# Selective scan in groups of three units: two inputs, then three scans on VectorE

## The chip, the cores and the metric

The kernel runs on one core of a Trainium2 chip. The metric is the time of one execution in microseconds (us) on the device. Engines are named as in the profile: PE (TensorE), DVE (VectorE), ACT (ScalarE), POOL (GpSimd) and SP, whose queue issues the DMAs here.

## What is computed

The reference is a block of four parts on an input of 4 images of 32x32 tokens with 384 channels: a convolution with a selective scan (four directions, 192 channels, 16 states), an attention without softmax, a router, and a mixture of eight experts. The change touches only the selective scan:

```python
dA = jnp.exp(d_t[..., None] * As)
h = h * dA + (d_t * u_t)[..., None] * B_t[:, :, None, :]
y = jnp.einsum('bkcn,bkn->bkc', h, C_t)
```

`h` runs along the 1024 positions of an image, for each channel and each of the 16 states apart; `y` sums `h * C` over the states.

## The kernel before

All parts are written with explicit semaphores, and each engine's order is written out by hand. The scan stage is a loop over 12 **tiles** (`NQ`): a tile has 128 partitions (64 channels of two images) and 1024 positions. Tiles 1 to 10 are a loop on the engine, whose waits take their values from registers; tiles 0 and 11 are written out, with constants. A tile has 32 **units** (`UN`): two directions (`dr`) of 16 states (`n`). One unit goes through five engines:

- PE copies the unit's row of B over the partitions, two matmuls into one of two PSUM slots, `B_PS[u % 2]` (`spread(q, u, 0, ...)`, the matmul at L1040), and the row of C into `C_PS` (`spread(q, u, 1, C_PS)`, also L1040).
- ACT computes the decay, `exp(delta * A)` (L762), and copies C from PSUM to SBUF (L767).
- DVE multiplies B in its slot with `delta * x` (the **input**, L1503) and then scans (L1510).
- POOL multiplies h with C (the **readout**, L546) for two units in one instruction.
- PE adds that product into `Y_PS` with an identity matmul (L1056), `LAG` = 5 units later (`add_trailing_y`). The first add of a tile is preceded by a matmul of the skip weights (L1053), which waits until ACT has emptied the previous tile's sum (`evacuate_y`, L743) and has written the diagonal (`skip_weights`, L739).

Ten units of a tile, those with `n` in `ON_POOL` = (1, 4, 7, 10, 13), get their input otherwise: SP loads the row of B from DRAM into one of five `xin` buffers, POOL multiplies it (`make_input`, L529), and the decay goes into the PSUM slot that B would have had. They are **POOL units** here, the other 22 **DVE units**.

Buffers bound how far the engines run apart: a PSUM slot comes free with the scan two units before (the wait on `sc_ok` ahead of `spread`), `C_PS` with ACT's copy of the unit before (`c_free`), and one of eight `hst` buffers with the Y add of eight units before (`ya_ok`, ahead of each scan). Each engine's queue is in order. On PE the order of a unit is B (DVE units only), C, Y of the unit five before. On DVE it is input, scan, unit by unit. On POOL (`read_outs`) it is, for each pair of units, the inputs of the POOL units four and five ahead and then the pair's readout.

Of the kernel before, what the change touches and what calls it, by code (L numbers as in the profile page):

```python
# [5 lines left out]
ALU = mybir.AluOpType  # L6
# [7 lines left out]
B, HW, C, DI, N, R, K = 4, 32, 384, 192, 16, 24, 4  # L14
# [6 lines left out]
NP = B // 2  # L21
NQ = NP * 2 * J
# [5 lines left out]
UN = 2 * N  # L28
HALF = S // 2
HALVES = 2 * OJ  # L30
# [2 lines left out]
DRING = 2  # L33
HRING = 8
LAG = 5
ON_POOL = (1, 4, 7, 10, 13)
LEAD = 4
XRING = 5
PADW = HW + 2
# [3 lines left out]
MADE = 4  # L43
# [40 lines left out]


def pool_units(u):
    return u // N * len(ON_POOL) + sum(n in ON_POOL for n in range(u % N))


POOL_UNITS = [u for u in range(UN) if u % N in ON_POOL]  # L90
VEC_UNITS = UN - len(POOL_UNITS)
assert VEC_UNITS % DRING == 0

# [19 lines left out]
def decay_slot(u):  # L113
    return (u - pool_units(u)) % DRING


def decay_before(u):

    vec = [v for v in range(-UN, UN) if v % UN not in POOL_UNITS]
    return vec[vec.index(u) - DRING]  # L120


assert len(POOL_UNITS) % XRING == 0

# [23 lines left out]
def hybrid_block_kernel(nc, a, out):  # L148
    with ExitStack() as ctx:
        def sem(name):  # L150
            return ctx.enter_context(nc.semaphore(name))
# [32 lines left out]
        dlt, dux = rb.take(2, S), rb.take(2, S)  # L184
# [26 lines left out]
        xin, decay = rs.take(XRING, S), rs.take(DRING, S)  # L211
        c_sb, hst = rs.take(RING, S), rs.take(HRING, S)
# [49 lines left out]
        def pair_of_banks(b):  # L262
            return ps[:, b:b + 2, :].rearrange("p b c -> p (b c)")
# [6 lines left out]
        B_PS = [pair_of_banks(0), pair_of_banks(2)]  # L270
# [24 lines left out]
        ab_ok, dm_st = sem("abs_ready"), [sem(f"delta_stored{i}") for i in range(MADE)]  # L295
        dl_ld, du_ld = [sem("delta_in0"), sem("delta_in1")], [sem("delta_x_in0"), sem("delta_x_in1")]
        rows_ok, rows_st, in_ok = sem("rows_copied"), [sem("rows_stored0"), sem("rows_stored1")], sem("input_on_pool")
# [4 lines left out]
        b_ok, c_ok, c_free, dec_ok = (sem(n) for n in ("b_spread", "c_spread", "c_copied", "decay_ready"))  # L302
        p1_ok, sc_ok, p2_ok, ya_ok, yev_ok = (sem(n) for n in ("input_ready", "scanned", "readout_ready", "y_added", "y_evacuated"))
# [32 lines left out]
        def settled(eng):  # L336


            eng.sem_inc(passed, 1)
# [3 lines left out]
        def _(sp):  # L343
# [50 lines left out]
            def load_delta(q, dr):  # L394
                sp.dma_start(dlt[:, dr], dl_dram[q * 2 + dr]).then_inc(dl_ld[dr], 16)
                sp.dma_start(dux[:, dr], du_dram[q * 2 + dr]).then_inc(du_ld[dr], 16)
# [20 lines left out]
            def b_row(q, u):  # L417
                dr, n = divmod(u, N)
                x = q * len(POOL_UNITS) + pool_units(u)
                if x >= XRING:  # L420
                    old_q, old = divmod(x - XRING, len(POOL_UNITS))
                    sp.wait_ge(sc_ok, old_q * UN + POOL_UNITS[old] + 3)
                for im in range(2):
                    sp.dma_start(xin[H2 * im:H2 * im + H2, x % XRING],
                                 b_dram[q // J, dr, im * N + n].partition_broadcast(H2)).then_inc(b_ld[x % XRING], 16)
# [5 lines left out]
            for i in range(MADE):  # L431
                sp.wait_ge(dm_st[i], NP * HALVES // MADE * 32)
            for U in range(NQ * UN):
                if U % N == FETCH_AT and N <= U < (2 * NQ - 1) * N:

                    half = U // N + 1
                    sp.wait_ge(sc_ok, U - FETCH_AT + 2)
                    load_delta(half // 2, half % 2)
                if U % UN in POOL_UNITS:
                    b_row(U // UN, U % UN)  # L440
                if U % (J * UN) == N and J * UN <= U < 3 * J * UN:
# [177 lines left out]
        def _(act):  # L619
# [87 lines left out]
            for p in range(NP):  # L707
# [13 lines left out]
                for s in range(HALVES + 1):  # L721
# [7 lines left out]
                    k, n = s // J + 1, s // J + 2  # L729
# [8 lines left out]
            def skip_weights(q):  # L738
                nc.scalar.activation(d_diag, ident, ACT.Identity, scale=d_sum[:, q % OJ, :]).then_inc(diag_ok, 1)  # L739

            def evacuate_y(q):
                act.wait_ge(ya_ok, q * UN + (UN + HRING))
                nc.scalar.activation(xy[:, q, :], Y_PS, ACT.Copy).then_inc(yev_ok, 1)  # L743

            def units(q, first, last):
                for u in range(UN):
                    dr, n = divmod(u, N)
                    U = q * UN + u
                    if n == 0:

                        act.wait_ge(dl_ld[dr], q * 16 + 16)

                    if u == LAG and not first:
                        evacuate_y(q - 1)
                        skip_weights(q)

                    held = u - 2 if n in ON_POOL else decay_before(u)
                    dst = B_PS[u % 2] if n in ON_POOL else decay[:, decay_slot(u)]
                    if not (first and held < 0):
                        act.wait_ge(sc_ok, q * UN + (held + 3))  # L760
                        settled(act)
                    nc.scalar.activation(dst, dlt[:, dr], ACT.Exp,  # L762
                                         scale=a_neg[:, q % OJ, dr, n:n + 1]).then_inc(dec_ok, 1)
                    act.wait_ge(c_ok, U + 1)

                    act.wait_ge(p2_ok, U + 1)
                    nc.scalar.activation(c_sb[:, u % RING], C_PS, ACT.Copy).then_inc(c_free, 1)  # L767
# [145 lines left out]
        def _(pe):  # L913
# [103 lines left out]
            for p in range(NP):  # L1017
# [9 lines left out]
                for s in range(HALVES):  # L1027
                    delta_product(p, s)
                    k, n = s // J + 1, s // J + 2
# [6 lines left out]
            def spread(q, u, m, dst):  # L1036

                dr, n = divmod(u, N)
                for h in range(2):
                    mm = pe.matmul(dst[:, h * 512:(h + 1) * 512], sel_lhs[0:BR, n],  # L1040
                                   bc[0:BR, q % OJ // J, dr, m, h * 512:(h + 1) * 512], start=True, stop=True)
                return mm
# [17 lines left out]
            def add_trailing_y(q, u, first):  # L1060
                if u >= LAG:
                    add_y(q, u - LAG)
                elif not first:
                    add_y(q - 1, UN - LAG + u)

            def tile_steps(q, first, last):
                if not first and not last:
                    pe.wait_ge(bc_ld, 16 * ((q + 1) // J + 1))
                for u in range(UN):
                    dr, n = divmod(u, N)  # L1070
                    U = q * UN + u

                    if n not in ON_POOL:
                        pe.wait_ge(sc_ok, U + 1)
                        spread(q, u, 0, B_PS[u % 2]).then_inc(b_ok, 1)
                    pe.wait_ge(c_free, U + 1)
                    spread(q, u, 1, C_PS).then_inc(c_ok, 1)
                    add_trailing_y(q, u, first)


            pe.wait_ge(ev_free, NP * FILLS)
# [244 lines left out]
        def _(dve):  # L1326
# [155 lines left out]
                        split_lo(p, k)  # L1482


            def scans(q, first, last):
                for u in range(UN):
                    dr, n = divmod(u, N)
                    U = q * UN + u
                    if n == 0:

                        dve.wait_ge(du_ld[dr], q * 16 + 16)
                    h, slot = hst[:, u % HRING], B_PS[u % 2]
                    if n in ON_POOL:
                        f, x = slot, xin[:, pool_units(u) % XRING]

                        dve.wait_ge(in_ok, q * len(POOL_UNITS) + (pool_units(u) + 1))
                        dve.wait_ge(dec_ok, U + 1)
                    else:
                        f, x = decay[:, decay_slot(u)], slot
                        seen = q * VEC_UNITS + (u - pool_units(u) + 1)  # L1500

                        dve.wait_ge(b_ok, seen)
                        nc.vector.tensor_tensor(x, x, dux[:, dr], ALU.mult).then_inc(p1_ok, 1)  # L1503

                        dve.wait_ge(p1_ok, seen)
                        dve.wait_ge(dec_ok, U + 1)
                    dve.wait_ge(ya_ok, U + 1)
                    if dr:
                        h, f, x = h[:, ::-1], f[:, ::-1], x[:, ::-1]
                    nc.vector.tensor_tensor_scan(h, f, x, 0.0, ALU.mult, ALU.add).then_inc(sc_ok, 1)  # L1510

            for i in range(MADE):
                dve.wait_ge(dm_st[i], NP * HALVES // MADE * 32)
            for k in range(2):
                dve.wait_ge(bc_st[k], K * NP // 2 * PLACED)
                dve.wait_ge(rows_st[k], K * NP // 2 * 16)
            scans(0, True, False)
            with nc.vector.Fori(1, NQ - 1) as q:
                scans(q, False, False)
            scans(NQ - 1, False, True)  # L1520

            def centre(c):
                dve.wait_ge(mean_ok, c + 1)
# [356 lines left out]
```

## Time and profile before

| | us |
|---|---|
| median of 3 runs (lowest to highest) | 2389.55 (2389.35 to 2389.83) |
| the profiled execution | 2390.58 |
| its span, first instruction to last | 2388.8 |
| busy in the span: PE, DVE, ACT, POOL | 2046.9, 1599.6, 1140.5, 1302.0 |

The profiled execution took 1.8 us more than its span and 1.0 us more than the median. The scan stage lies between about 302 and 1526 us of the span: a little over half of it. Busy time is the time in which an instruction of the engine runs; a row names the source line, and the idle time in front of it is put down to what released it.

### The profile page before, as it was taken

The numbers are of one execution on the slowest core, as the hardware profiler recorded it, in microseconds if no ns is written. First come the engines' busy times: TensorE is split into PE (matmuls) and PEld (weight loads), VectorE is DVE, ScalarE is ACT, GpSimd is POOL, SyncE is SP. The second block draws the span as 40 slices with busy tenths as digits, with TensorE's granted clock in tenths as the row PEclk, the third lists the DMA queues.
The fourth block names the chain that finished last, engine by engine and source line by source line (L and its number), as shares of the span: only waits on it lengthen the run. The fifth ranks groups of instructions, "written<-read, shape, count | busy, mean of one in ns | idle before, by whom it ended". The sixth has DMA issues, their size and how long they took to land.

```text
span 2388.8 us, 20259 instructions
## 1 busy us (share of the span) xinstructions
PE 2046.9 (86%) x5902; PEld 958.1 (40%) x5902; DVE 1599.6 (67%) x1480; ACT 1140.5 (48%) x1238; POOL 1302.0 (55%) x467
## 2 busy tenths in 40 slices
PE   6996578888888888888888888779997699999998
PEld 3432123333333333333333333236664355555554
DVE  5686989999999999999999999582556000000000
ACT  2684756666666666666666666312121111111111
POOL 0101079999999999999999999611222111111110
PEclk9987679999999999999999999899999899999999
DMA  5454533222333223233222231320223533333210
GB/s 213 173 192 124 217 80 109 76 61 61 75 88 88 70 61 75 66 97 83 61 61 61 81 95 36 159 88 8 74 86 128 199 118 119 119 116 119 98 43 6
DMA packets 78850, 231.98 MB, mean 97 GB/s; under 512 B 10783, under 2 KB 37009, under 8 KB 76880
## 3 DMA queue, kind: packets, MB, share of 16 engines
q1 hardware_dynamic: 72656, 214.39, 28.5%
q0 software_dynamic: 6144, 16.98, 2.0%
q8 instruction: 24, 0.39, 0.1%
q14 instruction: 26, 0.21, 0.0%
HBM read 169.24 MB, written 64.03 MB: 98 GB/s over the span
## 4 chain that ended last, share of the span: by engine, by line
PE 46%; DVE 32%; issue 12%; ACT 7%; DMA 1%; POOL 0%; DVEq 0%; ACTq 0%; SPq 0%; POOLq 0%
DVE arena L1510 18%; PE ps L1311 10%; PE ps L1299 10%; PE ps L1056 8%; DVE ps L1503 6%; PE ps L1040 3%; ACT ps L762 3%; PE ps L1247 3%; PE ps L955 2%; DVE arena L1385 1%; PE ps L1053 1%; PE ps L1198 1%; PE ps L1236 1%; PE ps L1176 1%; PE ps L982 1%
## 5 line engine op out<-in xcount | busy, mean ns | idle before, releaser
L546 POOL TENSOR_TENSOR arena<-arena 128x2048 f32<-128x2048 f32 x192 | 869.7, 4530 | 70.7 <-DVE arena L1510 70.6
L1056 PE MATMUL ps<-arena 128*128 128x512 f32 x1536 | 754.2, 615 | 3.3 <-POOL arena L546 3.2
L1510 DVE TENSOR_TENSOR_SCAN arena<-arena,ps 128x1024 f32<-128x1024 f32 x264 | 603.7, 2287 | 44.9 <-DVE ps L1503 23.5
L1040 PE MATMUL ps<-arena 96*128 (+1 forms) x1296 | 357.0, 391 | 209.1 <-DVE arena L1510 189.4
L767 ACT ACTIVATE arena<-ps 128x1024 f32<-128x1024 f32 x384 | 391.7, 1020 | 276.0 <-PE ps L1040 272.2
L1056 PEld LDWEIGHTS ps<-arena 128*128 128x128 f32 x1536 | 302.1, 197 | 268.0 <-issue 208.3
L529 POOL TENSOR_TENSOR arena<-arena 128x1024 f32<-128x1024 f32 x120 | 283.4, 2362 | 98.0 <-DMA arena<-b_rows 98.0
L1040 PEld LDWEIGHTS ps<-arena 96*128 96x128 bf16 x1296 | 118.7, 99 | 537.2 <-DVE arena L1510 298.9
L1503 DVE TENSOR_TENSOR ps<-ps,arena 128x1024 f32<-128x1024 f32 x264 | 318.8, 1208 | 5.6 <-DMA delta_x<-arena 2.9
L1782 DVE TENSOR_TENSOR arena<-ps,arena 128x384 f32<-128x384 f32 x32 | 17.9, 558 | 449.2 <-PE ps L1311 449.2
L762 ACT ACTIVATE arena<-arena 128x1024 f32<-128x1024 f32 x264 | 301.2, 1141 | 24.6 <-DVE arena L1510 24.6
L1510 DVE TENSOR_TENSOR_SCAN arena<-ps,arena 128x1024 f32<-128x1024 f32 x120 | 271.8, 2265 | 3.6 <-POOL arena L529 3.6
L605 POOL DMA_INDIRECT out<-arena x32 | 31.8, 994 | 436.0 <-DVE arena L1787 436.0
L1311 PE MATMUL ps<-arena 128*128 128x384 f32 x768 | 250.1, 486 | 0.0
L1299 PE MATMUL ps<-arena 128*128 128x512 f32 x576 | 249.0, 593 | 0.0
L1311 PEld LDWEIGHTS ps<-arena 128*128 128x128 f32 x768 | 145.4, 190 | 101.6 <-issue 3.8
L762 ACT ACTIVATE ps<-arena 128x1024 f32<-128x1024 f32 x120 | 134.2, 1119 | 106.7 <-DVE arena L1510 106.7
L1299 PEld LDWEIGHTS ps<-arena 128*128 128x128 f32 x576 | 109.7, 191 | 136.1 <-issue 133.7
L891 ACT ACTIVATE arena<-ps,arena 128x512 f32<-128x512 f32 x96 | 66.1, 689 | 175.8 <-PE ps L1299 175.8
L578 POOL TENSOR_TENSOR arena<-arena 128x384 f32<-128x384 f32 x32 | 27.0, 877 | 203.2 <-DVE arena L1624 203.2
L898 ACT ACTIVATE arena<-arena 128x384 f32<-128x384 f32 x32 | 16.8, 525 | 232.3 <-DVE arena L1782 232.3
L517 POOL COPY arena<-arena 128x1024 f32<-128x1024 f32 x6 | 13.4, 2238 | 190.8 <-ACT arena L648 190.8
(202 smaller groups left out, 1669.3 us busy)
## 6 DMA issues: line engine op xcount, KB each, us to landing
arena<-b_rows SPq DMA_DIRECT2D x240, 256.0 KB, 7.5
arena<-in_w SPq DMA_DIRECT2D x16, 2304.0 KB, 16.6
delta<-arena SPq DMA_DIRECT2D x24, 512.0 KB, 2.9
delta_x<-arena SPq DMA_DIRECT2D x24, 512.0 KB, 3.7
arena<-delta SPq DMA_DIRECT2D x24, 512.0 KB, 3.6
arena<-delta_x SPq DMA_DIRECT2D x24, 512.0 KB, 4.5
arena<-in_xT SPq DMA_DIRECT2D x6, 1536.0 KB, 9.8
slot_in<-arena SPq DMA_DIRECT2D x8, 772.0 KB, 13.7
```

Of the source, the lines that this page charges most:

```text
L529: nc.gpsimd.tensor_tensor(xin[:, x % XRING], xin[:, x % XRING], dux[:, dr], ALU.mult).then_inc(in_ok, 1)
L546: nc.gpsimd.tensor_tensor(hst[:, h:h + 2], hst[:, h:h + 2], c_sb[:, c:c + 2], ALU.mult).then_inc(p2_ok, 2)
L762: nc.scalar.activation(dst, dlt[:, dr], ACT.Exp, scale=a_neg[:, q % OJ, dr, n:n + 1]).then_inc(dec_ok, 1)
L767: nc.scalar.activation(c_sb[:, u % RING], C_PS, ACT.Copy).then_inc(c_free, 1)
L891: nc.scalar.activation(h_sb[:, m], ps[:, 3 + m % 3, :], ACT.Gelu_apprx_tanh, bias=b1_col[:, e, m:m + 1]).then_inc(hg_ok, 1)
L1040: mm = pe.matmul(dst[:, h * 512:(h + 1) * 512], sel_lhs[0:BR, n], bc[0:BR, q % OJ // J, dr, m, h * 512:(h + 1) * 512], start=True, stop=True)
L1056: mm = pe.matmul(Y_PS[:, h * 512:(h + 1) * 512], ident, hst[:, u % HRING, h * 512:(h + 1) * 512], start=False, stop=(u == UN - 1))
L1247: mm = pe.matmul(ps[:, attend_bank(i), 0:CA], xnT[:, b % 2, t, i * P:(i + 1) * P], w_eff[:, t], start=(t == 0), stop=(t == CT - 1))
L1299: mm = pe.matmul(ps[:, 3 + m % 3, :], w1[s][:, t, m * P:(m + 1) * P], xeT[:, s, t], start=(t == 0), stop=(t == CT - 1))
L1311: mm = pe.matmul(ps[:, 6 + i % 2, 0:C], h_sb[:, m, i * P:(i + 1) * P], w2[s][:, m], start=(m == 0), stop=(m == MT - 1))
L1503: nc.vector.tensor_tensor(x, x, dux[:, dr], ALU.mult).then_inc(p1_ok, 1)
L1510: nc.vector.tensor_tensor_scan(h, f, x, 0.0, ALU.mult, ALU.add).then_inc(sc_ok, 1)
```

## The change

The POOL units of a tile become every third one, 2, 5, ..., 29: ten again, so 22 DVE units remain, of which 30 and 31 form a last group of two. DVE's program is cut in two functions. For each group of three it issues the inputs of both DVE units and then the three scans. PE follows: within a group it spreads B, C of the first unit, B of the second, then one Y add, C, Y add, C of the third, Y add. The number of instructions of each kind is what it was. `decay_slot`, `decay_before` and POOL's program are not edited, but follow `POOL_UNITS`. DVE's wait on the stored deltas ahead of the stage is gone (its first input still waits for `delta_x` to be loaded).

```diff
-ON_POOL = (1, 4, 7, 10, 13)
+GROUP = 3
...
 def pool_units(u):
-    return u // N * len(ON_POOL) + sum(n in ON_POOL for n in range(u % N))
+    return u // GROUP
...
-POOL_UNITS = [u for u in range(UN) if u % N in ON_POOL]
+POOL_UNITS = list(range(GROUP - 1, UN, GROUP))
...
-                    held = u - 2 if n in ON_POOL else decay_before(u)
-                    dst = B_PS[u % 2] if n in ON_POOL else decay[:, decay_slot(u)]
+                    held = u - 2 if u in POOL_UNITS else decay_before(u)
+                    dst = B_PS[u % 2] if u in POOL_UNITS else decay[:, decay_slot(u)]
...
-                    if n not in ON_POOL:
+                    at = u % GROUP
+                    if u not in POOL_UNITS:
                         pe.wait_ge(sc_ok, U + 1)
                         spread(q, u, 0, B_PS[u % 2]).then_inc(b_ok, 1)
+                    if at == 1:
+                        add_trailing_y(q, u - 1, first)
                     pe.wait_ge(c_free, U + 1)
                     spread(q, u, 1, C_PS).then_inc(c_ok, 1)
-                    add_trailing_y(q, u, first)
+                    if at:
+                        add_trailing_y(q, u, first)
...
-            for i in range(MADE):
-                dve.wait_ge(dm_st[i], NP * HALVES // MADE * 32)
...
+            def scans(q):
+
+                for g in range(0, UN, GROUP):
+                    units = range(g, min(g + GROUP, UN))
+                    for u in units:
+                        if u not in POOL_UNITS:
+                            input_of(q, u)
+                    for u in units:
+                        scan(q, u)
```

`input_of(q, u)` waits for B (`b_ok`) and multiplies; `scan(q, u)` has the waits and the scan of before.

In DVE's queue, in tile 0, from unit 0 on, before (L1503 is an input, L1510 a scan; the scan with `arena<-ps,arena` is that of a POOL unit):

```order
208 L1510 SCALAR_TENSOR_TENSOR arena<-arena,ps 128x1024 [waits y_added,decay_ready,input_ready]
209 L1510 SCALAR_TENSOR_TENSOR arena<-ps,arena 128x1024 [waits y_added,decay_ready,input_on_pool]
210 L1503 TENSOR_TENSOR ps<-ps,arena 128x1024 [waits b_spread]
211 L1510 SCALAR_TENSOR_TENSOR arena<-arena,ps 128x1024 [waits y_added,decay_ready,input_ready]
212 L1503 TENSOR_TENSOR ps<-ps,arena 128x1024 [waits b_spread]
213 L1510 SCALAR_TENSOR_TENSOR arena<-arena,ps 128x1024 [waits y_added,decay_ready,input_ready]
```

The same place now (L1496 is an input, L1513 a scan; the first row of tile 0 is input 0):

```order
208 L1496 TENSOR_TENSOR ps<-ps,arena 128x1024 [waits b_spread]
209 L1513 SCALAR_TENSOR_TENSOR arena<-arena,ps 128x1024 [waits y_added,decay_ready,input_ready] x2
210 L1513 SCALAR_TENSOR_TENSOR arena<-ps,arena 128x1024 [waits y_added,decay_ready,input_on_pool]
211 L1496 TENSOR_TENSOR ps<-ps,arena 128x1024 [waits b_spread] x2
212 L1513 SCALAR_TENSOR_TENSOR arena<-arena,ps 128x1024 [waits y_added,decay_ready,input_ready] x2
213 L1513 SCALAR_TENSOR_TENSOR arena<-ps,arena 128x1024 [waits y_added,decay_ready,input_on_pool]
```

No scan stands right behind its own input any more: another input lies between.

In PE's queue, in the loop's body, units 3 to 5 of a tile before (L1040 with `scanned` is B, with `c_copied` C; L1056 is a Y add):

```order
308 L1074 REGISTER_ALU
309 L1040 MATMUL ps<-arena 128x512 [waits scanned]
310 L1040 MATMUL ps<-arena 128x512
311 L1040 MATMUL ps<-arena 128x512 [waits c_copied]
312 L1040 MATMUL ps<-arena 128x512
313 L1054 REGISTER_ALU
314 L1056 MATMUL ps<-arena 128x512 [waits readout_ready]
315 L1056 MATMUL ps<-arena 128x512
```

And units 3 and 4 now:

```order
308 L1075 REGISTER_ALU
309 L1040 MATMUL ps<-arena 128x512 [waits scanned]
310 L1040 MATMUL ps<-arena 128x512
311 L1040 MATMUL ps<-arena 128x512 [waits c_copied]
312 L1040 MATMUL ps<-arena 128x512
313 L1075 REGISTER_ALU
314 L1040 MATMUL ps<-arena 128x512 [waits scanned]
315 L1040 MATMUL ps<-arena 128x512
316 L1054 REGISTER_ALU
317 L1056 MATMUL ps<-arena 128x512 [waits readout_ready]
318 L1056 MATMUL ps<-arena 128x512
```

B of the group's second unit has moved ahead of the Y add that used to stand before it, and all three Y adds of the group are queued behind its wait.

## Rows read from the trace of the kernel before

**Rows 1.** Window of 100 us: length, busy us (count) of PE, PEld, DVE, ACT, POOL, clock, DMA, GB/s
```profile
500.00:600.00 100.00, 84.38 (x238) 35.22 (x237) 95.68 (x55) 66.16 (x66) 94.03 (x26) 0.97 0.27 73
```
**Rows 2.** Groups of instructions, shapes apart: busy, mean ns | idle before, releasers
```profile
L546 POOL TENSOR_TENSOR arena<-arena 128x2048 f32<-128x2048 f32 x192 | 869.7, 4530 | 70.7 <-DVE arena L1510 70.6
L1510 DVE TENSOR_TENSOR_SCAN arena<-arena,ps 128x1024 f32<-128x1024 f32 x264 | 603.7, 2287 | 44.9 <-DVE ps L1503 23.5 <-ACT ps L762 15.1 <-PE ps L1056 3.8
L1503 DVE TENSOR_TENSOR ps<-ps,arena 128x1024 f32<-128x1024 f32 x264 | 318.8, 1208 | 5.6 <-DMA delta_x<-arena 2.9 <-PE ps L1040 2.7
L1510 DVE TENSOR_TENSOR_SCAN arena<-ps,arena 128x1024 f32<-128x1024 f32 x120 | 271.8, 2265 | 3.6 <-POOL arena L529 3.6
```
**Rows 3.** Timeline of DVE: the first scans of tiles 6 and 7
```profile
913.39 2.29 DVE L1510 TENSOR_TENSOR_SCAN arena<-arena,ps 128x1024 f32<-128x1024 f32 x1 [0.20 <-ACT ps L762]
1014.54 2.29 DVE L1510 TENSOR_TENSOR_SCAN arena<-arena,ps 128x1024 f32<-128x1024 f32 x1 [0.20 <-ACT ps L762]
```
**Rows 4.** Timeline of DVE in the loop: start, us, what, idle before
```profile
1000.15 1.21 DVE L1503 TENSOR_TENSOR ps<-ps,arena 128x1024 f32<-128x1024 f32 x1
1001.54 2.29 DVE L1510 TENSOR_TENSOR_SCAN arena<-arena,ps 128x1024 f32<-128x1024 f32 x1 [0.19 <-ACT ps L762]
1003.75 2.27 DVE L1510 TENSOR_TENSOR_SCAN arena<-ps,arena 128x1024 f32<-128x1024 f32 x1
1005.93 1.21 DVE L1503 TENSOR_TENSOR ps<-ps,arena 128x1024 f32<-128x1024 f32 x1
```
**Rows 5.** Timeline of DVE in tile 11, outside the loop
```profile
1424.39 1.21 DVE L1503 TENSOR_TENSOR ps<-ps,arena 128x1024 f32<-128x1024 f32 x1
1425.64 2.29 DVE L1510 TENSOR_TENSOR_SCAN arena<-arena,ps 128x1024 f32<-128x1024 f32 x1
```
**Rows 6.** Timeline of DVE ahead of the stage: two products independent of each other
```profile
294.93 1.22 DVE L1430 TENSOR_TENSOR arena<-arena 128x1024 f32<-128x1024 f32 x1
296.08 1.22 DVE L1423 SCALAR_TENSOR_TENSOR arena<-arena 128x1024 f32<-128x1024 f32 x1
```
**Rows 7.** Timeline at the stage's start: POOL's first inputs and unit 1's scan
```profile
307.54 4.64 POOL L529 TENSOR_TENSOR arena<-arena 128x1024 f32<-128x1024 f32 x2 [97.99 <-DMA arena<-b_rows]
309.92 2.29 DVE L1510 TENSOR_TENSOR_SCAN arena<-ps,arena 128x1024 f32<-128x1024 f32 x1 [3.62 <-POOL arena L529]
```
**Rows 8.** Timeline of PE in the loop: spreads (two pairs), Y add, spreads
```profile
1003.89 1.04 PE L1040 MATMUL ps<-arena 96*128 x4 [1.89 <-DVE arena L1510]
1004.76 1.88 PE L1056 MATMUL ps<-arena 128*128 128x512 f32 x4
1006.48 1.03 PE L1040 MATMUL ps<-arena 96*128 x4
```
**Rows 9.** Timeline at the change of tiles: ACT, PE, and DVE's wait behind them
```profile
1024.77 1.01 ACT L743 ACTIVATE arena<-ps 128x1024 f32 x1
1025.67 0.40 ACT L739 ACTIVATE arena<-arena 128x128 f32<-128x128 f32 x1
1025.96 1.15 ACT L762 ACTIVATE arena<-arena 128x1024 f32<-128x1024 f32 x1
1032.26 1.03 PE L1040 MATMUL ps<-arena 96*128 x4
1032.90 1.23 DVE L1503 TENSOR_TENSOR ps<-ps,arena 128x1024 f32<-128x1024 f32 x1 [0.91 <-PE ps L1040]
```
**Rows 10.** Timeline of POOL in the loop: readout, input, readout
```profile
1000.45 4.53 POOL L546 TENSOR_TENSOR arena<-arena 128x2048 f32<-128x2048 f32 x1 [0.61 <-DVE arena L1510]
1004.95 2.37 POOL L529 TENSOR_TENSOR arena<-arena 128x1024 f32<-128x1024 f32 x1
1007.27 4.52 POOL L546 TENSOR_TENSOR arena<-arena 128x2048 f32<-128x2048 f32 x1
```
**Rows 11.** Windows of 4 us in the loop, columns as in rows 1
```profile
848.00:852.00 4.00, 2.33 (x7) 0.86 (x5) 3.81 (x3) 3.10 (x3) 3.22 (x1) 1.00 0.00 0
852.00:856.00 4.00, 3.78 (x7) 1.66 (x8) 3.81 (x4) 2.06 (x2) 4.00 (x3) 0.59 0.00 0
```

More of the change, by code:

```diff
@@ L1482, in _ @@
                         split_lo(p, k)
[L1485 to L1510, printed above, removed]
@@ L1512, in _, with input_of, scan @@
-            for i in range(MADE):
-                dve.wait_ge(dm_st[i], NP * HALVES // MADE * 32)
+            def input_of(q, u):
+                dr, x = u // N, B_PS[u % 2]
+                seen = q * VEC_UNITS + (u - pool_units(u) + 1)
+                if u % N == 0:
+                    dve.wait_ge(du_ld[dr], q * 16 + 16)
+                dve.wait_ge(b_ok, seen)
+                nc.vector.tensor_tensor(x, x, dux[:, dr], ALU.mult).then_inc(p1_ok, 1)
+            def scan(q, u):
+                dr, U = u // N, q * UN + u
+                h, slot = hst[:, u % HRING], B_PS[u % 2]
+                if u in POOL_UNITS:
+                    f, x = slot, xin[:, pool_units(u) % XRING]
+                    dve.wait_ge(in_ok, q * len(POOL_UNITS) + (pool_units(u) + 1))
+                else:
+                    f, x = decay[:, decay_slot(u)], slot
+                    dve.wait_ge(p1_ok, q * VEC_UNITS + (u - pool_units(u) + 1))
+                dve.wait_ge(dec_ok, U + 1)
+                dve.wait_ge(ya_ok, U + 1)
+                if dr:
+                    h, f, x = h[:, ::-1], f[:, ::-1], x[:, ::-1]
+                nc.vector.tensor_tensor_scan(h, f, x, 0.0, ALU.mult, ALU.add).then_inc(sc_ok, 1)
@@ L1516, in _ @@
                 dve.wait_ge(rows_st[k], K * NP // 2 * 16)
-            scans(0, True, False)
+            scans(0)
             with nc.vector.Fori(1, NQ - 1) as q:
-                scans(q, False, False)
-            scans(NQ - 1, False, True)
+                scans(q)
+            scans(NQ - 1)
             def centre(c):
```

## The prediction

> **What bounds the kernel now.** I read the windows first: in 100 us of the stage DVE is busy 95.7 us, POOL 94.0, PE 84.4, ACT 66.2 [rows 1]. The groups then say who waits. DVE's scans were idle before for 44.9 us in all, and the row puts most of that down to DVE's own input (23.5) and to ACT's exp (15.1), while the inputs waited only 2.7 us for PE; POOL's readouts waited 70.6 us for DVE's scans [rows 2]. So DVE is the bound, and the others wait for it. The timeline shows what DVE's 101.15 us per tile [rows 3] are made of. From an input's start to its own scan's start 1.39 us pass in the loop [rows 4] and 1.25 in tile 11 [rows 5], though the input lasts 1.21. From a scan to the next instruction it is 2.21 or 2.18 us, less than the scan's 2.29 or 2.27 [rows 4]: an instruction that needs nothing of the one before starts 0.08 us before that one ends. 22 x 1.39 + 32 x 2.20 = 101.0 us, the tile's period. There is no other wait in a tile of the loop. The exp that rows 2 and 4 name ended just when the input did; it isn't a second cost, since the 1.39 is the same where ACT is not named.
>
> **The change, term by term.**
>
> 1. *The dependent start goes.* A scan now has another input between itself and its own. The trace before has no input followed by something independent of it; the bounds are the input's whole 1.21 us from above, and 1.21 less the overlap seen elsewhere, 0.07 for two independent products (296.08 - 294.93 = 1.15 of 1.22 us) [rows 6] to 0.08, from below. I take 1.14, since rows 6 are the same engine with an instruction nearly as short. Gain: 10 tiles x 22 x (1.39 - 1.14) = 55.0 us, and 2 x 22 x (1.25 - 1.14) = 4.8: **59.8 us**. With 1.21 it is 41.4, with 1.13 it is 62.5. The 0.14 us that the loop has over tile 11 I read as register work and further waits that come one after another once the input is done; now they can run under the second input.
>
> 2. *The first POOL unit.* Unit 1's scan waited 3.62 us for POOL's input, which began at 307.54 [rows 7]. Now unit 2 is the first; its input is ready at 309.9, as before. DVE was free at 306.3 after an input and a scan (1.25 + 2.2); now it does two of each first (2 x 1.14 + 2 x 2.2 = 6.7), and is free at 309.5. The wait shrinks to 0.4: **3.2 us gained**.
>
> 3. *The steady group, on the other engines.* A group takes DVE 2 x 1.14 + 3 x 2.20 = 8.9 us (9.4 before). Count from the end of the last scan of the group before. DVE starts its inputs at -0.1 and 1.05, the scans at 2.2, 4.4 and 6.6. B of the second unit, call it B2, needs the very scan that ends at 0. PE started 0.06 us after a scan's end (1001.54 + 2.29 to 1003.89) [rows 4, 8], and an input started 0.64 after its spread did (1032.90 - 1032.26) [rows 9]: B2 is usable at 0.70, wanted at 1.05. That holds if PE is free at 0. A pair of spreads takes 0.43 us, half of the 0.87 between rows 8's first starts, and a Y add 1.72 (1004.76 to 1006.48) [rows 8]. PE thus has B2 0.1 to 0.5, Y to 2.2, C to 2.6, Y to 4.4, C to 4.8, Y to 6.5, then the next group's first B when the second scan ends (6.7) to 7.2, and C to 7.6. It is idle until 8.9, 1.3 us to spare and 0.35 more before DVE waits. ACT's exp of the POOL unit waits for the scan that ends at 4.5 and takes 1.15 [rows 9] and is done at about 5.8, wanted at 6.6. Cost: nothing. If PE came later than those 1.65 us, DVE would wait for each us beyond.
>
> 4. *The change of tiles.* Before the third Y add of the second group stands the skip matmul, and it needs ACT's two steps, which need the old tile's last Y add. In that group the old tile's last Y starts at 2.6 and ends, 1.88 later [rows 8], at 4.5; ACT's L743 follows, L739 ends 1.30 us after L743's start and the next exp starts 1.19 after it [rows 9]. So PE gets the diagonal at 6.0, the skip matmul (like a Y add, 1.72) and the Y add go to 9.5, and B of the next group is usable at 10.15 where DVE wants it at 8.8. The exp of the third unit starts at 5.8 and ends at 6.9, 0.3 late, a part of the same wait. Before, such waits summed to 2.7 us in the stage [rows 2]. Eleven changes x 1.35 = **15 us lost**. Ends: 0, if LAG's slack takes it up, and 25.
>
> 5. *POOL.* Start to start a readout takes 4.50 us and an input 2.32 [rows 10]: 16 x 4.50 + 10 x 2.32 = 95.2 us per tile. DVE's tile becomes 22 x 1.14 + 32 x 2.20 + 1.35 = 96.8. Six units cost POOL 3 x 4.50 + 2 x 2.32 = 18.1 us and DVE 17.8: inside a tile POOL falls back 0.3 us per six units, 1.7 over thirty, and recovers over the last two units, which hold no POOL unit. PE's third Y add of each second group is the one that meets it, at 4.8; it may come at 6.5. Walked through, the readout is done at 5.0 early in the tile and 6.0 late. Cost 0, with half a us of air.
>
> 6. *The clock.* In some windows PE ran part of the time at half speed, the lower level of 1.2 GHz: the granted clock was 0.59 in one whose predecessor had PE busy only 2.33 of 4 us [rows 11]. A stretch of some 3 us costs PE 1.6 us, just the slack of term 3. I put **3 us** for those that fall on a tile's change. Idle stretches of PE get shorter, from 1.9 us [rows 8] to 1.3, so I expect no more of them.
>
> The dropped wait on stored deltas costs and gives nothing: the first input still waits for `delta_x` (2.9 us in rows 2), loaded after those stores. SP's row loads and delta loads are issued at the same units give or take one; five buffers are ten or more units ahead.
>
> Sum: -59.8 - 3.2 + 15 + 3 = -45.0 us. The profiled execution took 2390.6, which gives 2345.6; the median of the runs is 1.0 lower: **2345 us**.
>
> **Rivals.**
>
> *All of it arrives* (0.12). The change of tiles costs nothing: 2389.6 - 63.0 = 2327 us. For it: before, the inputs waited 2.7 us for PE in the whole stage [rows 2]. Against: term 4's chain is 1.3 us longer than its place.
>
> *POOL paces* (0.15). Scans now come in bursts, pairs do not fit triples, and POOL's readout idles now and then as it does now (101.15 - 95.2 = 6 us per tile). If half of that stays, a tile takes 98.2: 10 x 2.95 + 5 for the other two tiles + 3 = 37 us gained, 2352 us.
>
> *The start isn't set by the dependence* (0.06). An input would take 1.39 us to any successor, because DVE needs that time between two instructions of this kind; term 1 is then 0, term 4 shrinks to about 0.8 x 11 = 9, and the time is 2389.6 - 3.2 + 9 = 2395 us. Against it stand the 2.18 and 2.21 us after scans, with the same waits, and rows 6.
> The Trainium skill, "VectorE: DVE Perf Modes", section "The DRAIN you can't avoid", speaks for this one: the next operation waits until the pipe is empty whatever the semaphores do, so one should cut operations, not waits. By that rule reordering would bring nothing; the overlap of 0.08 us in rows 4 already disagrees with it.
>
> *PE comes late to B2, slower than before* (0.07). Place: the wait on the scan ahead of B2, with three Y adds behind it. If PE is still in a Y add when the scan ends, DVE's second input waits up to 1.72 - 0.35 = 1.4 us in each of 132 groups: 181 us, 2526 us. It decides from (59.8 + 3.2) / 132 = 0.48 us per group. A cause could be the clock: at half speed PE's three Y adds and five spread pairs take 2 x 7.3 = 14.6 us a group, against DVE's 8.9. Against it: the 1.3 us to spare.
>
> **How the numbers follow.** The forecast has 0.60; its own range is 2335 to 2356, from the ends of term 4 and a value of 1.17 in term 1. A measurement here tells 0.2% (4.8 us). The range that leaves out two in ten takes in the first rival and POOL's, and 1.21 in term 1: 2327 to 2366. Faster 0.88: the forecast, the first two rivals and a small part of the others. Same 0.03, slower 0.09.
>
> **What would show it.** Right: input to input and input to scan 1.13 to 1.15 us; a tile in the loop 96 to 98 us; DVE's idle before scans named by its own input nearly gone; a wait for PE of about 1 us at the input of unit 6, once a tile, and none at the second input of a group; POOL's idle before readouts down from 70 to about 20 us. Wrong: intervals near 1.39, waits at each group's second input, readouts without idle time and PE waiting for them, or a granted clock well under 0.97 in the stage.

## The result, and the profile after

| | before | after |
|---|---|---|
| median (lowest to highest), us | 2389.45 (2388.55 to 2389.83), 4 runs | 2348.74 (2346.89 to 2350.89), 4 runs |
| profiled execution, us | 2390.58 | 2349.24 |
| span, us | 2388.8 | 2347.4 |

The ratio is 0.9826 (95% interval 0.9813 to 0.9839): 41 us less, where 45 were forecast. The groups of instructions of the kernel after, columns as in [rows 2]:

```profile
L546 POOL TENSOR_TENSOR arena<-arena 128x2048 f32<-128x2048 f32 x192 | 865.9, 4523 | 2.9 <-DVE arena L1513 2.9
L1056 PE MATMUL ps<-arena 128*128 128x512 f32 x1536 | 732.5, 599 | 59.9 <-POOL arena L546 59.8
L1513 DVE TENSOR_TENSOR_SCAN arena<-arena,ps 128x1024 f32<-128x1024 f32 x264 | 587.9, 2268 | 0.0
L529 POOL TENSOR_TENSOR arena<-arena 128x1024 f32<-128x1024 f32 x120 | 283.0, 2358 | 128.9 <-DMA arena<-b_rows 128.9
L1496 DVE TENSOR_TENSOR ps<-ps,arena 128x1024 f32<-128x1024 f32 x264 | 309.9, 1219 | 28.5 <-PE ps L1040 28.2
L1513 DVE TENSOR_TENSOR_SCAN arena<-ps,arena 128x1024 f32<-128x1024 f32 x120 | 271.9, 2266 | 7.9 <-ACT ps L762 4.2 <-POOL arena L529 3.4 <-issue 0.4
```

The DVE units' scans (L1513, before L1510) had 44.9 us of idle time in front of them and now have none. The inputs (L1496, before L1503) had 5.6 and now have 28.5, nearly all for PE. On POOL things turned round: its readouts waited 70.7 us for DVE and now 2.9, but its inputs wait 128.9 us for the DMA of their rows, where they waited 98.0. Those 98 us are the time before the stage; the other 31 are new. PE's Y adds now wait 59.9 us for POOL, before 3.3. So POOL, which waited for DVE, is now waited for.

DVE in a steady group, the answer to [rows 4] (start, us, what; `x2` is two in a row):

```profile
916.80 2.34 DVE L1496 TENSOR_TENSOR ps<-ps,arena 128x1024 f32<-128x1024 f32 x2
919.05 4.46 DVE L1513 TENSOR_TENSOR_SCAN arena<-arena,ps 128x1024 f32<-128x1024 f32 x2
923.42 2.27 DVE L1513 TENSOR_TENSOR_SCAN arena<-ps,arena 128x1024 f32<-128x1024 f32 x1
925.60 2.34 DVE L1496 TENSOR_TENSOR ps<-ps,arena 128x1024 f32<-128x1024 f32 x2
```

The two inputs take 2.25 us from start to start of what follows, 1.13 each, and the group 8.80. Over the loop the means are 1.127 from an input to the next and 1.131 from an input to a scan; before, 1.404 from an input to its scan (1.244 in the two tiles outside the loop).

The change of tiles, the answer to [rows 9]:

```profile
902.23 1.02 ACT L743 ACTIVATE arena<-ps 128x1024 f32 x1 [0.81 <-PE ps L1056]
903.15 0.39 ACT L739 ACTIVATE arena<-arena 128x128 f32<-128x128 f32 x1
903.44 1.11 ACT L762 ACTIVATE ps<-arena 128x1024 f32<-128x1024 f32 x1
903.81 1.98 PE L1053 MATMUL ps<-arena 128*128 x4 [1.30 <-ACT arena L739]
904.59 2.29 DVE L1513 TENSOR_TENSOR_SCAN arena<-ps,arena 128x1024 f32<-128x1024 f32 x1 [0.42 <-ACT ps L762]
905.62 1.88 PE L1056 MATMUL ps<-arena 128*128 128x512 f32 x4
```
```profile
907.98 2.36 DVE L1496 TENSOR_TENSOR ps<-ps,arena 128x1024 f32<-128x1024 f32 x2 [1.10 <-PE ps L1040]
```

This is the chain of term 4: evacuation, diagonal, exp of unit 5, skip matmul, and DVE waits 0.42 us at the scan of unit 5 and 1.10 at the input of unit 6, 1.52 us in each tile of the loop.

What was not forecast stands ahead of it in the same tile. SP and POOL:

```profile
888.78 0.33 SPq L395 DMA_DIRECT2D arena<-delta  x1
889.14 0.43 SPq L396 DMA_DIRECT2D arena<-delta_x  x1
889.62 4.96 SPq L424 DMA_DIRECT2D arena<-b_rows  x8
890.76 4.51 POOL L546 TENSOR_TENSOR arena<-arena 128x2048 f32<-128x2048 f32 x1
897.69 2.36 POOL L529 TENSOR_TENSOR arena<-arena 128x1024 f32<-128x1024 f32 x1 [2.41 <-DMA arena<-b_rows]
900.01 9.00 POOL L546 TENSOR_TENSOR arena<-arena 128x2048 f32<-128x2048 f32 x2
```

The old tile's last scan ended at 888.75. The delta loads wait for it and went out at 888.78, and the row of B of unit 5 stands behind them in SP's queue. It was issued at 889.62, and POOL's input, which needs it, began at 897.69 after 2.41 us of idle time. At the start of each of the tiles 1 to 10 POOL's input began 8.4 to 9.8 us after that scan's end and had idled 1.9 to 3.7 us. Before, unit 4 was the POOL unit, issued ahead of the delta loads.

POOL never makes up for that wait: apart from the row it waits for nothing in the loop, and most tiles last its 95.0 us of work and its wait. Late in the tile its readouts come too late for PE, and PE for DVE. One of the longest such waits, at unit 30 of tile 2 (the last line is a window, columns as in [rows 1], the clock in it 0.75):

```profile
585.12 2.93 PE L1056 MATMUL ps<-arena 128*128 128x512 f32 x4 [1.80 <-POOL arena L546]
588.95 2.42 DVE L1496 TENSOR_TENSOR ps<-ps,arena 128x1024 f32<-128x1024 f32 x2 [1.79 <-PE ps L1040]
```
```profile
584.00:588.00 4.00, 2.88 (x5) 1.11 (x6) 3.16 (x2) 2.10 (x3) 4.00 (x2) 0.75 0.00 0
```

PE had stood idle for 1.80 us until 585.12; from 586.02 on the granted clock was at its lower level, 0.5 or 1.2 GHz, for a short stretch. DVE's waits for PE at the inputs of units 24 and 30 sum to 14.3 us in the stage, and the five of 1.5 us and more, 9.4 us of the 14.3, all lie at such a stretch; each of these five stretches began 0.4 to 1.2 us after the end of a wait of PE for POOL of 1.8 us. DVE's other waits at these two units last at most 0.4 us.

### The profile page after: what moved, and what is told of

It is laid out like the page before. It is cut to its first block, busy times and chain, and to the rows that moved or that the text cites. A ratio compares the mean times of both kernels' runs of the same rounds, so it can differ in the third digit from the quotient of the medians.

```text
span 2347.4 us, 20258 instructions
## 1 busy us (share of the span) xinstructions
PE 2031.5 (87%) x5902; PEld 940.8 (40%) x5902; DVE 1577.5 (67%) x1480; ACT 1141.0 (49%) x1238; POOL 1298.9 (55%) x467
## 3 DMA queue, kind: packets, MB, share of 16 engines
q1 hardware_dynamic: 72656, 214.39, 29.1%
## 4 chain that ended last, share of the span: by engine, by line
PE 46%; DVE 18%; issue 15%; POOL 14%; ACT 5%; DMA 1%; ACTq 0%; DVEq 0%; POOLq 0%; SPq 0%
PE ps L1315 11%; PE ps L1303 11%; DVE arena L1513 10%; POOL arena L546 9%; PE ps L1056 7%; POOL arena L529 5%; PE ps L1251 3%; PE ps L1040 2%; PE ps L955 2%; ACT arena L767 1%; DVE arena L1389 1%; DVE ps L1496 1%; PE ps L1053 1%; PE ps L982 1%; PE ps L1202 1%
## 5 line engine op out<-in xcount | busy, mean ns | idle before, releaser
L1056 PE MATMUL ps<-arena 128*128 128x512 f32 x1536 | 732.5, 599 | 59.9 <-POOL arena L546 59.8
L1513 DVE TENSOR_TENSOR_SCAN arena<-arena,ps 128x1024 f32<-128x1024 f32 x264 | 587.9, 2268 | 0.0
L1040 PE MATMUL ps<-arena 96*128 (+1 forms) x1296 | 366.6, 387 | 115.0 <-DVE arena L1513 94.0
L1056 PEld LDWEIGHTS ps<-arena 128*128 128x128 f32 x1536 | 287.8, 190 | 324.1 <-issue 193.8
L529 POOL TENSOR_TENSOR arena<-arena 128x1024 f32<-128x1024 f32 x120 | 283.0, 2358 | 128.9 <-DMA arena<-b_rows 128.9
L1496 DVE TENSOR_TENSOR ps<-ps,arena 128x1024 f32<-128x1024 f32 x264 | 309.9, 1219 | 28.5 <-PE ps L1040 28.2
L1040 PEld LDWEIGHTS ps<-arena 96*128 96x128 bf16 x1296 | 116.3, 99 | 444.0 <-issue 188.2
L1513 DVE TENSOR_TENSOR_SCAN arena<-ps,arena 128x1024 f32<-128x1024 f32 x120 | 271.9, 2266 | 7.9 <-ACT ps L762 4.2
L1303 PE MATMUL ps<-arena 128*128 128x512 f32 x576 | 249.0, 593 | 0.0
L1315 PEld LDWEIGHTS ps<-arena 128*128 128x128 f32 x768 | 145.4, 190 | 101.6 <-issue 3.8
L1303 PEld LDWEIGHTS ps<-arena 128*128 128x128 f32 x576 | 109.6, 191 | 136.1 <-issue 133.7
```

The costliest lines, as they stand in the source:

```text
L529: nc.gpsimd.tensor_tensor(xin[:, x % XRING], xin[:, x % XRING], dux[:, dr], ALU.mult).then_inc(in_ok, 1)
L1056: mm = pe.matmul(Y_PS[:, h * 512:(h + 1) * 512], ident, hst[:, u % HRING, h * 512:(h + 1) * 512], start=False, stop=(u == UN - 1))
L1303: mm = pe.matmul(ps[:, 3 + m % 3, :], w1[s][:, t, m * P:(m + 1) * P], xeT[:, s, t], start=(t == 0), stop=(t == CT - 1))
L1315: mm = pe.matmul(ps[:, 6 + i % 2, 0:C], h_sb[:, m, i * P:(i + 1) * P], w2[s][:, m], start=(m == 0), stop=(m == MT - 1))
```

## Experiments

All ran beside the kernel before, whose own median was 2389.4 to 2391.4 from one set of runs to the next, so that small differences are read from the ratios. The medians are of 4 to 10 runs each.

| run | median, us | ratio to before (95%) | loop tile, us |
|---|---|---|---|
| after (the change) | 2348.7 | 0.9826 (0.9813 to 0.9839) | 97.0 to 99.6 |
| rows first | 2333.4 | 0.9763 (0.9747 to 0.9779) | 96.4 |
| skip later | 2345.1 | 0.9807 (0.9791 to 0.9824) | 97.1 to 99.4 |
| both | 2317.8 | 0.9698 (0.9682 to 0.9714) | 95.2 |
| PE's old order | 2363.1 | 0.9890 (0.9874 to 0.9907) | 98.4 to 99.3 |
| units only | 2398.6 | 1.0029 (1.0018 to 1.0041) | 101.3 to 102.9 |
| wait back | 2351.1 | 0.9828 (0.9812 to 0.9844) | 96.5 to 99.2 |
| units, rows first | 2401.1 | 1.0033 (1.0020 to 1.0045) | 101.1 to 102.9 |
| both, PE old | 2357.4 | 0.9857 (0.9840 to 0.9873) | 98.3 |
| units, rows first, skip later | 2386.9 | 0.9991 (0.9981 to 1.0001) | 101.1 to 102.1 |
| both, PE old, skip with unit 3 | 2338.2 | 0.9781 (0.9763 to 0.9798) | 96.9 |

**Rows first.** SP's two steps of a unit change places:

```diff
 for U in range(NQ * UN):
+    if U % UN in POOL_UNITS:
+        b_row(U // UN, U % UN)
     if U % N == FETCH_AT and N <= U < (2 * NQ - 1) * N:
...
-    if U % UN in POOL_UNITS:
-        b_row(U // UN, U % UN)
```

> The changed kernel, but SP issues the row of B of unit 5 of each half tile ahead of the two delta loads instead of behind them. Theory (POOL paces: its tile is 95.2 us of work plus the 2 to 3.7 us that it waits for that row; its lag is what makes PE late at units 24 and 30): POOL's idle time put down to the row's DMA falls from 129 to about 98 us (the start alone), the 0.4 us waits of DVE for PE at the inputs of units 24 and 30 go, those of 1.5 to 2.1 us shrink, the tile falls from 97.3 to about 96.5 us, the time from 2349 to about 2336. Rival (those waits come from pairs against triples and from the clock, and the row only fills idle time): POOL idles elsewhere, tile 97.3, 2346 or more.

(The edit moves the row of unit 5 alone: the other delta loads are issued at unit 21, which has no row.) 15.3 us less than the change, and 2333.4 where about 2336 was expected. In the loop POOL no longer waits for a row, and DVE waits at the change of tiles alone (waits of DVE and of POOL, 400 to 1400 us: in total, times, longest):

```profile
DVE ps L1496 <- PE ps L1040: 11.9, 11, 1.1
DVE arena L1513 <- ACT ps L762: 4.2, 10, 0.4
```
```profile
POOL arena L546 <- DVE arena L1513: 13.1, 11, 1.2
```

The waits at units 24 and 30 are gone, the long ones too. The theory stands: they came from POOL's lag. The stretches of low clock went with them. The kernel after had four in the loop, this run has none, and its granted clock is 1.00 in the whole loop.

**Skip later.** The skip matmul joins the sum with unit 4, and ACT writes its diagonal one unit later:

```diff
+SKIP_AT = 4
...
-                if u == 0:
+                if u == SKIP_AT:
...
-                        pe.matmul(Y_PS[:, h * 512:(h + 1) * 512], d_diag, xy[:, q, h * 512:(h + 1) * 512], start=True, stop=False)
+                        pe.matmul(Y_PS[:, h * 512:(h + 1) * 512], d_diag, xy[:, q, h * 512:(h + 1) * 512], start=False, stop=False)
...
-                                   start=False, stop=(u == UN - 1))
+                                   start=(u == 0), stop=(u == UN - 1))
...
                         evacuate_y(q - 1)
+                    if u == LAG + 1 and not first:
                         skip_weights(q)
```

> The changed kernel, but the skip weights' matmul is added with unit 4 instead of ahead of unit 0, and ACT writes the diagonal one unit later. Both theories: the waits at the third scan and at the input of unit 6 (0.42 and 1.10 us a tile, 15 to 17 us in all) go nearly to zero. Theory (POOL paces the tile at 95.2 + 2.1 = 97.3): the time returns as waits at units 24 and 30, and the kernel gains under 4 us: 2345 to 2349. Rival (DVE's chain at the change of tiles is on the path): 2349 - 15 = 2334.

3.6 us less, and the ranges overlap (2340.6 to 2350.4 against 2346.9 to 2350.9); 2345.1 lies in the theory's range. The profiled execution is the slowest of the four. In it DVE's waits for PE did not shrink, they spread:

```profile
DVE ps L1498 <- PE ps L1042: 25.6, 37, 3.7
```
```profile
POOL arena L530 <- DMA arena<-b_rows: 30.9, 11, 3.9
POOL arena L547 <- DVE arena L1515: 0.8, 1, 0.8
```

The first row is of DVE, 25.6 us against 25.1 in the kernel after over the same 1000 us; the others are of POOL, which still waits for its row and for next to nothing else. Its own work is 95.0 us a tile, its wait for the row 2 to 4, and most tiles are their sum. The 1.10 us at unit 6 are gone from most tiles; waits of 0.3 to 0.4 us stand at units 12, 18, 24 and 30, and the longest, up to 3.7 us at unit 6 and 1.7 at unit 30, lie at the seven stretches of low clock in its loop. The times of its executions go with the clock: the mean granted clock was 0.954 in the slowest and 0.957 in the fastest. So the 3.6 us are a rough figure.

**Both.**

> Both edits of the two runs before. Theory (two bounds nearly equal, each hides the other): more than the sum of the single gains; tile at POOL's 95.2 to 95.7 us, time 2322 to 2328. Rival (they are independent): the sum of the single gains.

2317.8 us, 31.0 less than the change where the single gains add up to 18.9, and 3% less than the kernel before. The tile came out as expected, 95.2 us; the time lies 4 us below the expected range. This is the fastest version of the study, and its loop too has no stretch of low clock. A window of the stage, columns as in [rows 1]:

```profile
500.00:600.00 100.00, 87.32 (x252) 35.48 (x251) 99.83 (x58) 71.36 (x71) 99.89 (x29) 1.00 0.32 85
```

DVE and POOL are both busy all the time (99.8 and 99.9 us of 100): 22 x 1.13 + 32 x 2.19 = 94.9 us of DVE and 95.0 of POOL in a tile of 95.2. By these rows a shorter tile would need less work on both; that was not tried.

**PE's old order**, with DVE's groups kept:

```diff
-                    if at == 1:
-                        add_trailing_y(q, u - 1, first)
                     pe.wait_ge(c_free, U + 1)
                     spread(q, u, 1, C_PS).then_inc(c_ok, 1)
-                    if at:
-                        add_trailing_y(q, u, first)
+                    add_trailing_y(q, u, first)
```

> The changed kernel with PE's old order: B, C, Y add, unit by unit; DVE's groups are kept. By the walk through a group the Y add in front of the group's second B ends 0.4 us after the scan that B waits for, so that B is usable at 1.07 where DVE wants it at 1.05: theory (PE's new order is worth little): 2349 to 2360, waits of 0 to 0.1 us at second inputs. Rival (PE's new order carries the gain, since the Y adds wait for POOL): 0.3 us or more at each second input, 2385 or more.

2363.1: 14.3 us more, just above the first range and far below the second. The waits of DVE over 1000 us of the stage:

```profile
DVE ps L1493 <- PE ps L1040: 29.1, 66, 1.4
```

They were 25.1 us in 31 waits with the new order. From a group's first input to its second it was 1.44 us in the mean instead of 1.13. Of the 29.1 us, 13.5 are one wait of 1.35 us in each tile, at the input of unit 7, whose B is the second one behind the skip matmul. The run mixes POOL's lag with PE's order, so the order was tried again without the lag.

**Both, PE old**, the same edit on the fastest version:

> The fastest version so far (rows first, skip matmul later; 2317.8) with PE's old order, B, C, Y add unit by unit. Theory (B of the second unit comes late by itself, since a Y add stands before it: its input started 0.24 us late in most groups of the run with PE's old order): 0.2 to 0.25 us in each of 132 groups, 2344 to 2351, tile 97.5 or more. Rival (those waits came from POOL's late row and the skip matmul, which are gone here): 2318 to 2324.

2357.4, 6 us beyond the theory's range, and mostly not for its reason. Most groups lose 0.07 us and two in each tile some 0.35; 1.70 us a tile sit in one place, the input of unit 10:

```profile
530.55 1.23 DVE L1495 TENSOR_TENSOR ps<-ps,arena 128x1024 f32<-128x1024 f32 x1 [1.70 <-PE ps L1042]
```

In this order the Y add of unit 4, and with it the moved skip matmul, stands right ahead of B of unit 10, a second unit. So the placement was undone:

> PE's old order with rows first, and the skip matmul with unit 3 instead of unit 4, so that it no longer stands right ahead of B of a group's second unit (there it cost 1.70 us a tile). Theory (PE's old order costs 0.07 us in every group and 0.35 us twice a tile at the second input, 17 to 20 us in all, beside that placement): 2334 to 2340. Rival (the skip matmul costs 1.7 us wherever it stands in this order, since PE has no slack left): 2352 or more.

2338.2, inside the theory's range. PE's new order is thus worth about 20 us in the fastest version (each order with the better of the two places tried for the skip matmul). Over 1000 us of the stage 40 inputs wait, each of them the second of its group (units 1, 19, 25 and 31):

```profile
DVE ps L1495 <- PE ps L1042: 11.5, 40, 0.4
```

The rest is time too short to be listed as a wait: the second input starts at least 1.18 us after the first in this order, 1.11 in the other.

**Units only.** The kernel before with every third unit on POOL (`ON_POOL` and its uses replaced by `POOL_UNITS`); DVE and PE go unit by unit.

> The kernel before with one thing of the change: the POOL units are every third one. DVE and PE go unit by unit as before. Theory (the gain is all in DVE's order): input to own scan stays at 1.40 us in the loop, the tile at 101.2 us, time 2387 to 2391; POOL waits for its late row now, but has 6 us of slack a tile. Rival (the even spacing of the POOL units gives part of the gain): 2380 or less.

Both were wrong: 8 us slower, and the ratio's interval lies above 1. POOL waited about 4 us for its row in each tile, and DVE 1.1 us for PE at the input of unit 6 in eight of the loop's ten tiles, as these waits over 1000 us of the stage show:

```profile
DVE ps L1503 <- PE ps L1040: 9.1, 9, 1.1
```
```profile
POOL arena L529 <- DMA arena<-b_rows: 41.1, 10, 5.0
POOL arena L546 <- DVE arena L1510: 29.5, 43, 1.3
```

I took POOL's wait for the row for the cause of DVE's wait.

**Units, rows first.**

> The kernel before with every third unit on POOL, unit by unit, and the row of B issued ahead of the delta loads. Theory (the 8 us that the even spacing cost are the late row of unit 5 alone: POOL waited 4 us for it in each tile, and DVE 1.1 us at unit 6 behind it): POOL's wait for the row goes, the tile is 101.2 us again, 2388 to 2391. Rival (the spacing itself, with the skip matmul at unit 5, makes the wait at unit 6): 2395 or more, tile 102.5.

2401.1, 10 us more than the kernel before. The row came in time, and the wait stayed, again in eight of ten tiles:

```profile
931.63 2.29 DVE L1510 TENSOR_TENSOR_SCAN arena<-ps,arena 128x1024 f32<-128x1024 f32 x1 [0.21 <-ACT ps L762]
935.02 1.23 DVE L1503 TENSOR_TENSOR ps<-ps,arena 128x1024 f32<-128x1024 f32 x1 [1.10 <-PE ps L1040]
```

The theory fell; the rival, which named the skip matmul, was left.

**Units, rows first, skip later.**

> The run with every third unit on POOL, unit by unit, rows first, and now also the skip matmul with unit 4 (before it: with unit 0). Theory (what the even spacing costs is the change of tiles: ACT's two extra steps stand ahead of the exp of unit 5, which is a POOL unit now, and PE's skip matmul behind them ahead of B of unit 6): the 1.1 us wait at the input of unit 6 goes, the tile is 101.1 to 101.3 us, 2388 to 2391. Rival (the spacing costs elsewhere, as at the scan of unit 9, 0.3 us a tile): 2395 or more.

2386.9, 1 us below the theory's range and the kernel before again (the interval holds 1). The wait at unit 6 is gone from the loop. In five of its ten tiles DVE waits 0.8 us instead at the input of unit 10, behind the moved skip matmul:

```profile
DVE ps L1505 <- PE ps L1042: 4.0, 5, 0.8
```

Where that wait is missing the tile lasts 101.1 to 101.4 us, as before. So the even spacing costs 8 to 10 us, nearly all of it at the change of tiles, and brings no gain that these runs tell. That the exp behind ACT's two extra steps is then that of a POOL unit is a likely reason, not a tested one. Input to own scan is still 1.40 us here. Why the same steps cost the old spacing almost nothing was not separated further.

**Wait back.** DVE's wait on `dm_st` ahead of the stage returns to the changed kernel.

> The changed kernel with DVE's wait on the stored deltas put back ahead of the first input. Theory (the wait is worth nothing, since unit 2's scan waits for POOL's first row in any case): DVE's first input starts 3.5 us later and unit 2's scan when it did; 2348 to 2350. Rival (the 3.5 us are gained at the end): 2352.

2351.1 (2346.8 to 2355.1) against 2348.7 (2346.9 to 2350.9), ratios 0.9828 and 0.9826: no difference that these runs tell. The first input started 4.0 us later and again waited 2.9 us, and unit 2's scan waited 0.7 instead of 3.4 and started 1.3 later.

## Why the prediction was right, and where not

The time, 2348.7, lies in the range of 2327 to 2366 and 4 us from the forecast. The likeliest case named the right gain. That it came so near is partly luck: the gain of term 1 came 6 us larger than forecast and almost 3 us more are in no term, and this made up for most of the 12 us by which the losses of POOL and the clock were forecast too small.

1. *The dependent start* was right in kind and a little small. 220 x (1.404 - 1.129) = 60.5 us in the loop and 44 x (1.244 - 1.129) = 5.1 outside, **65.6** against 59.8. The value taken for the interval, 1.14, measured 1.13. The reading of the loop's extra time as register work is borne out by the trace of the kernel before: behind the input that ended at 1001.35 it has a register instruction at 1001.39 and a semaphore wait at 1001.48, and the scan at 1001.54; behind the input of tile 11 the scan starts after 0.04 us. The rule weighed for the third rival (the Trainium skill, "VectorE: DVE Perf Modes", section "The DRAIN you can't avoid") was told without its last part. The Trainium skill says there that the next operation does not start before the pipe is empty, and then that one that isn't held starts earlier. The trace agrees with the second: an input that lasts 1.21 us was followed after 1.12. The runs with the new units but DVE's old order leave 1.40, so the gain is the regrouping's.

2. *The first POOL unit*: forecast 3.2, and the idle rows give 3.2 (2.9 of the wait for `delta_x` and 0.3 at the scan), but by another way. The row `delta_x<-arena` reads out<-in: it is the store of `delta_x`, not its load, and so the removed wait on the stored deltas. Costing the removal at nothing because "the first input still waits for `delta_x`" was a misread row (with the wait back, the 2.9 us return). The sum was right all the same, since from unit 2's scan on all hangs on POOL's first row.

3. *The steady group* held: groups of 8.80 us without a wait in the middle of each tile, B of the second unit in time. The run with PE's old order says what that ordering carries.

4. *The change of tiles*: forecast 15. The inputs of unit 6 waited 13.1 us, where 2.7 had stood before, and the scans of unit 5 4.6: **15.0 us** more, in the place and by the chain described. But taking it away alone gave 3.6.

5. *POOL* is the step that failed: "Cost 0", with "SP's row loads and delta loads are issued at the same units give or take one; five buffers are ten or more units ahead". The buffers are, the queue is not, and the one unit decides. The row of unit 5 stands behind delta loads that wait for the old tile's last scan. POOL's 95.0 us became 97 to 99.6, its lag reached PE's Y adds late in the tile, and DVE waited at units 24 and 30, **14.3 us**, and 0.8 at others. It is a circle: the row waits for DVE's scan, POOL for the row, PE for POOL, DVE for PE. One of the prediction's own signs of being wrong came with it: "readouts without idle time and PE waiting for them". The readouts' idle time is 2.9 us where 20 were foreseen, and PE waited 59.9. The rival that had POOL pace the kernel (2352) was nearer on this point, though it gave another reason.

6. *The clock*: forecast 3 us. The four waits of 1.5 to 2.1 us in the loop and the one in the last tile are some 7.4 us longer than five of the usual 0.4, and all fell where the granted clock over the 8 us before was about 0.8. Low clock alone does not cost that: the kernel before had 21 such stretches in its loop, and its inputs waited 2.7 us for PE in the whole stage. The kernel after had four, and they came with PE's wait for POOL. So a slow stretch cost much only where POOL's lag had used up PE's slack; the rows-first run, without lag and without slow stretches, can't tell the two apart.

Sum by measured terms: -65.6 - 3.2 + 15.0 + 15.1 = -38.7 us, where 15.1 is POOL's and the clock's (28.2 - 13.1, all waits of inputs for PE but those of unit 6). The spans differ by 41.4. Of the 2.7 us left, 1.1 lie behind the last scan (870.9 us against 872.0) and 0.6 ahead of the first input, apart from its wait. The rest, 1 us, lies in the starts of what follows a scan.

Two bounds near each other (POOL with its late row, about 97.3 us a tile, and DVE with its change of tiles, 94.9 + 1.5 = 96.4) explain why 3.6 and 15.3 became 31.0: with both lifted the tile is 95.2. A scan of a DVE unit lasts 2.268 us now and 2.287 before. The other runs place it: 2.286 to 2.287 in the three with DVE's old order, 2.268 to 2.270 in all with its new one. It goes with the regrouping, and a scan that starts while another instruction still runs is the shorter one (a POOL unit's scan lasts 2.291 us right after a wait, 2.263 otherwise). Why is open.

## What to carry to other kernels

When an in-order engine pays for its own result, look for one independent instruction to put between; here it gave 0.27 us for each of 220 products in the loop. Before costing a reordering of consumers at nothing, walk the queue that feeds them: in this kernel a row came only after what its queue waited for in front of it, though five buffers stood ready. And when an edit at a visible wait brings little, try it together with the next one before dropping it.

## What the runs showed of the hardware

From the start of a Vector product of 1.21 us to a scan that needs it, 1.24 us pass where the waits are constants, 1.40 in the loop where they come from registers; to an instruction that doesn't need it, 1.13 in both. So the extra 0.16 us of the loop were hidden wholly by one instruction in between. The two row loads of 256 KB issued right behind the delta loads (512 KB each) were usable after about 8.1 us (889.62 to 897.69). TensorE's granted clock fell to its lower level after the engine had waited 1.80 us for POOL (583.32 to 585.12, clock 0.5 from 586.02 on), though not after every wait of that length; in the loops of the runs in which DVE and POOL were kept busiest (rows first, both) it was 1.00 throughout.
